# Attention in rounds of two tiles: four shared score accumulators, and the shared work laid out anew over the steps

## The reference, cut to what matters

```
y = layernorm(x1)                          # 512 x 512
q, k = y @ Wq, y @ Wk                      # 8 heads of 64 columns
gl_v, gl_o = y @ Ws, y @ Wd                # 8 heads x 5 experts each
wv   = top2_mask(gl_v) * sigmoid(gl_v)
v    = sum over e of wv[..., e] * (y @ Wv[e])        # 8 heads x 64
attn = softmax(q * 64**-0.5 @ k.T) @ v
out  = sum over e of top2_mask(gl_o)[..., e] * attn @ Wo[e]
x    = x1 + tanh(g) * out
```

## Time and profile before

| | us |
|---|---|
| median of 3 runs | 1353.11 |
| the profiled execution | 1354.09 |
| its span | 1352.3 |
| PE busy in the span | 1245.2 |
| DVE busy | 855.2 |
| POOL busy | 696.3 |
| ACT busy | 638.3 |

### The profile page before, as it was taken

One profiled execution on the slowest core, in us unless ns is written; L12 is line 12 of the kernel. 1 busy time (PEld: TensorE's weight loads), 2 busy tenths in 40 slices (PEclk: granted clock), 3 DMA queues, 4 the chain that ended last, 5 costly groups with the idle time before them and its releaser, 6 DMA issues.

```text
span 1352.3 us, 20097 instructions
## 1 busy us (share of the span) xinstructions
PE 1245.2 (92%) x6376; PEld 909.4 (67%) x6376; DVE 855.2 (63%) x1587; ACT 638.3 (47%) x1402; POOL 696.3 (51%) x499
## 2 busy tenths in 40 slices
PE   3899999999999997889899999999999999999985
PEld 2688888888888876656566566576576575675653
DVE  5677776868777562754755765666666566466453
ACT  3343443434344323455545555555554554564551
POOL 2524242434424242654863963963954945955853
PEclk8799999999999998999999999999999999999997
DMA  6231313223131233001010010010020020010010
GB/s 221 74 110 47 116 62 100 93 94 109 47 116 39 86 141 110 19 0 32 1 63 31 0 62 31 0 62 31 0 90 3 8 85 0 8 54 0 23 39 32
DMA packets 40713, 75.73 MB, mean 56 GB/s; under 512 B 3760, under 2 KB 4272, under 8 KB 40688
## 3 DMA queue, kind: packets, MB, share of 16 engines
q1 hardware_dynamic: 40688, 75.42, 16.7%
HBM read 58.63 MB, written 16.78 MB: 56 GB/s over the span
## 4 chain that ended last, share of the span: by engine, by line
PE 36%; POOL 15%; issue 5%; DVE 3%; ACT 1%; POOLq 1%; DVEq 0%; ACTq 0%
PE ps_r L1577 7%; PE ps_r L1589 6%; POOL v_acc L1171 5%; PE ps_o L1652 5%; PE ps_p L1640 5%; PE ps_s L1629 5%; PE ps_r L1612 5%; POOL spare L1165 4%; POOL z L1183 4%; POOL v_acc L1165 1%; PE ps_r L1566 1%; PE ps_r L1603 1%; DVE sig L1434 1%; DVE nmax L1348 1%; PE ps_r L1596 0%
## 5 line engine op out<-in xcount | busy, mean ns | idle before, releaser
L1348 DVE TENSOR_REDUCE nmax<-ps_s 128x1 f32<-128x512 f32 x256 | 173.9, 685 | 207.3 <-PE ps_s L1629 207.2
L1226 ACT ACTIVATE probs<-ps_s,nmax 128x512 f32<-128x512 f32 x256 | 176.4, 689 | 262.0 <-DVE nmax L1348 259.3
L1183 POOL TENSOR_TENSOR z<-z,z_tmp 128x1280 f32<-128x1280 f32 x56 | 163.7, 2923 | 155.3 <-DVE z_tmp L1362 142.7
L1171 POOL TENSOR_TENSOR v_acc<-v_acc,spare 128x512 f32<-128x512 f32 x128 | 165.7, 1294 | 10.0
L1629 PE MATMUL ps_s<-k,q 64*128 64x512 f32 x768 | 123.7, 426 | 47.1 <-ACT probs L1226 45.6
L1640 PEld LDWEIGHTS ps_p<-ident,probs 128*128 128x128 f32 x1024 | 115.5, 142 | 73.0 <-issue 52.5
L1640 PE MATMUL ps_p<-ident,probs 128*128 128x128 f32 x1024 | 160.2, 283 | 1.7 <-ACT pt L1235 1.7
L1235 ACT ACTIVATE pt<-ps_p 128x512 f32<-128x512 f32 x256 | 151.9, 594 | 3.6 <-PE ps_p L1640 3.6
L1165 POOL TENSOR_TENSOR spare<-xv,pick 128x512 f32<-128x512 f32 x128 | 136.3, 1065 | 10.0
L1629 PEld LDWEIGHTS ps_s<-k,q 64*128 64x128 f32 x768 | 62.5, 185 | 101.6 <-ACT probs L1226 60.1
L1652 PE MATMUL ps_o<-pt,v_acc 128*64 128x512 f32 x512 | 130.6, 611 | 0.2 <-ACT pt L1235 0.2
(11 more groups left out here) (165 smaller groups left out, 2196.7 us busy)
## 6 DMA issues: line engine op xcount, KB each, us to landing
stage<-in_x SPq DMA_DIRECT2D x32, 256.0 KB, 3.1
stage<-in_ctx SPq DMA_DIRECT2D x32, 256.0 KB, 2.7
x_sb<-in_x SPq DMA_DIRECT2D x8, 1024.0 KB, 5.2
x_dram<-x_sb SPq DMA_DIRECT2D x32, 256.0 KB, 2.0
stage<-x_dram SPq DMA_DIRECT2D x8, 1024.0 KB, 5.6
spare<-x_dram SPq DMA_DIRECT2D x8, 1024.0 KB, 5.7
out_dram<-spare SPq DMA_DIRECT2D x32, 256.0 KB, 2.0
stage<-in_ctx_t SPq DMA_DIRECT2D x28, 256.0 KB, 3.3
```

Source lines behind the costliest of these rows:

```text
L1171: pool.tensor_tensor(acc, acc, v_tmp[:], ALU.add).then_inc(v_steps, 1)
L1183: pool.tensor_tensor(zv, zv, z_tmp[:, h % 2], ALU.add).then_inc(z_pool, 1)
L1226: act.activation(probs[:, n % PROBS, :], ps_s[:, n % 2, :], ACT.Exp, bias=nmax[:, n:n + 1], accum_out=den[:, h, t:t + 1]).then_inc(p_exp, 1)
L1348: dve.tensor_reduce(nmax[:, n:n + 1], ps_s[:, n % 2, :], AX_X, ALU.max, negate=True).then_inc(nmax_ready, 1)
```

## The change

All is in `expert_attention`. What it does:

- `ps_p` goes; `ps_s` has four banks, one a tile. A tile's transposed exponentials are written into the bank that held its scores. Scores wait until the copies of the tiles two rounds before are done (`pt_ready`), no more for an exponential.
- A round is two steps. On even n PE issues `scores(n)`, then the transposes of tiles n-2 and n-1, ACT the copies of n-2 and n-1 and then the exponentials of n and n+1, and DVE the maxima of n and n+1, all at the head of the step. On odd n there is only shared work.
- `values` is one block of 16 matmuls at step 12 of the pair.
- The tables of shared parts are new. High parts are taken in the step in which a part ends, low parts always in the odd step of the round.
- Gates: one `compare` for both kinds, 8 larger operations at step 1 with other slices, one count over both at step 2, and all of `route_values` at step 3.
- POOL: all `mix_values` of a batch, then the sums of heads 1 to 5. The sums of heads 6 and 7 go to DVE (`mix_sum`), at steps 41 and 42; `turn_z` is at step 43 and waits for these.

```diff
-    TURN_Y_AT = [-11, -11, -10, -9]
-    EXPERTS_AT = [[-9], [-8, -7], [-5, -4], [-3]]
-    Q_AT = [[-6, -6], [1, 2], [6, 6], [18, 18]]
-    K_AT = [[-3, -2], [3, 4], [10, 10], [19, 19]]
-    PV_AT = [11, 12, 12, 13]
-    TURN_O_AT = [17, 25, 34, 41]
-    TURN_Z_AT = [45, 45, 45]
-    RESULT_AT = [[46], [47], [47, 48], [49]]
+    TURN_Y_AT = [-11, -11, -10, -10]
+    EXPERTS_AT = [[-9], [-8], [-2], [-1, 0]]
+    Q_AT = [[-6, -5], [1, 2], [7, 8], [17]]
+    K_AT = [[-3], [3, 6], [9, 10], [18, 19]]
+    PV_AT = 12
+    TURN_O_AT = [16, 23, 31, 39]
+    TURN_Z_AT = [43, 43, 43]
+    RESULT_AT = [[45], [46], [47], [48]]
     NORMALISE_AT = -13
-    GATES_AT = -3
-    ROUTE_AT = [-1, -1]
-    MASK_AT = 1
+    GATES_AT = 1
+    ROUTE_AT = 3
     MIX_PLACES = [(1, 1), (2, 0)]
+    LAST_SUMS = [(2, 1), (3, 0)]
+    BANKS = 4
...
-                if n or not first:
-                    pe.wait_ge(p_exp, b * STEPS + n)
+                if n >= BANKS or not first:
+                    pe.wait_ge(pt_ready, b * STEPS + n + 2 - BANKS)
...
-                if part == 1 and 0 <= n - LAG < STEPS:
-                    turn_probs(b, n - LAG, first)
+                if part == 1 and n % 2 == 0:
+                    for before in (n - 2, n - 1):
+                        if 0 <= before < STEPS:
+                            turn_probs(b, before)
...
+            def batch(b, first=False):
+                for p in range(PAIRS):
+                    mix_values(b, p, first)
+                for p in range(LAST_PAIR):
+                    mix_sums(b, p)
...
+            def mix_sum(b, h):
+                dve.wait_ge(z_dve, b * H + h + 1)
+                if h == 2 * LAST_PAIR:
+                    dve.wait_ge(z_pool, (b + 1) * POOL_SUMS)
+                else:
+                    dve.wait_ge(z_ready, b * 2 + 1)
+                zv = z[:].rearrange("p t (e k) -> p t e k", e=E)
+                dve.tensor_tensor(zv, zv, z_tmp[:, h % 2], ALU.add).then_inc(z_ready, 1)
...
+            def compare(b):
+                dve.wait_ge(logits_ready, b * NT + NT)
+                both = logits[:].rearrange("p s g e -> p (s g) e")
+                square = beaten[:].rearrange("p g k j -> p g (k j)")
+                for d in range(1, E):
+                    early, late = both[:, :, 0:E - d], both[:, :, d:E]
+                    for first_place, other, than, order in ((d, late, early, ALU.is_gt), (d * E, early, late, ALU.is_ge)):
+                        places = square[:, :, bass.ds(first_place, E - d, step=E + 1)]
+                        dve.tensor_tensor(places, other, than, order).then_inc(compared, 1)
```

More of the change, by code:

```diff
@@ L925, in ended, with lo_behind @@
         return [what[:2] for what in parts_at(n) if what[2] == what[3] - 1]
-    def steps_behind(behind, name, i):
-        return behind.get(name + "0", 1) if name in "qk" and i == 0 else behind.get(name, 1)
+    def lo_behind(n):
+        return 1 - n % 2
     RING = 3
@@ L1035, in expert_attention @@
         z_pool = sem("z_pool")
+        z_ready = sem("z_ready")
         zt_ps = sem("zt_ps")
@@ L1280, in step @@
                             out_copy(b, p, first)
[L1281 to L1284, removed]
-                    return
[L1286 to L1291, removed]
+                    if n % 2 == 0:
+                        for before in (n - 2, n - 1):
+                            if 0 <= before < STEPS:
+                                probs_copy(b, before, first)
+                        for tile in (n, n + 1):
+                            if 0 <= tile < STEPS:
+                                scores_exp(b, tile, first)
+                    return
+                for name, i in ended(n):
+                    part_hi(b, name, i, first)
                 if n == NORMALISE_AT:
@@ L1299, in _ @@
             for n in range(EARLY - STEPS, EARLY):
-                for part in range(3):
+                for part in range(2):
                     step(0, n, part, True)
@@ L1460, in step @@
                     for what in ended(n - behind):
-                        if behind == steps_behind(LO_BEHIND, *what):
+                        if behind == lo_behind(n - behind):
                             part_lo(b, *what)
                 if part == 3:
[L1464 to L1469, removed]
+                    if n == GATES_AT:
+                        compare(b)
+                    if n == GATES_AT + 1:
+                        count_better(b)
                         count_values(b)
-                    if n == ROUTE_AT[1]:
+                    if n == ROUTE_AT:
                         route_values(b, first)
[L1473 to L1476, removed]
                     if n == NORMALISE_AT:
@@ L1632, in scores, with turn_probs, values @@
                             end.then_inc(s_ready, 1)
-            def turn_probs(b, n, first):
+            def turn_probs(b, n):
                 pe.wait_ge(p_exp, b * STEPS + n + 1)
-                if n >= 2 or not first:
-                    pe.wait_ge(pt_ready, b * STEPS + n - 1)
                 for k in range(NT):
-                    end = pe.transpose(ps_p[:, n % 2, k, :], probs[:, n % PROBS, k * P:(k + 1) * P], ident[:])
+                    end = pe.transpose(ps_s[:, n % BANKS, k * P:(k + 1) * P], probs[:, n % BANKS, k * P:(k + 1) * P],
+                                       ident[:])
                 end.then_inc(pt_ps, 1)
[L1643 to L1655, removed]
+            def values(b, p, first):
+                pe.wait_ge(pt_ready, b * STEPS + PAIR * p + PAIR)
+                pe.wait_ge(v_steps, (b * PAIRS + p + 1) * V_STEPS)
+                if p or not first:
+                    pe.wait_ge(o_ready, b * PAIRS + p)
+                for k in range(NT):
+                    for a in range(2):
+                        end = pe.matmul(ps_o[head_rows(a), :], v_acc[:, p, k, a, :], pt[:, p % 2 * 2 + a, k, :],
+                                        start=k == 0, stop=k == NT - 1)
+                end.then_inc(o_ps, 1)
             def step(b, n, part, first=False, last=False):
@@ L1660, in step @@
                     scores(b, n, first)
[L1661 to L1662 removed]
+                if part == 1 and n % 2 == 0:
+                    for before in (n - 2, n - 1):
+                        if 0 <= before < STEPS:
+                            turn_probs(b, before)
                 if part == 2:
                     for p in range(PAIRS):
[L1665 to L1667 removed]
+                        if n == PAIR * p + PV_AT:
+                            values(b, p, first)
                     for what in parts_at(n):
```

91 lines of the change are left out of this document (35 added, 56 removed).

## The result

The change made the kernel slower: 1389.81 us (median of 4 runs, 1388.45 to 1393.8) against 1352.82 in the same comparison, a ratio of 1.0276 with a 95% interval of 1.0251 to 1.0300. I had forecast 1340 and given 1308 to 1364.

What follows compares the result with a forecast made beforehand. PE was taken as the bound, busy 92.6 of 98.1 us a batch. Terms 4.1 - 10 - 2 - 2.8 - 2.6 = -13.3 from 1353.1 gave 1340 us, range 1308 to 1364.

Steps and rivals of the forecast that it cites:

- PE work, 90.0 us a batch: Second half, steady batch: PE work falls from 92.6 to 90.0 us, by joined values groups and fewer interruptions.
- rival 3: The PE work doesn't shrink, a batch stays at 92.6 us of it: 1359 us, chance 0.13.
- All three waits of scores for exponentials go: Second half: with four score banks all three pauses of scores go, 4.5 us a batch.
- The gates: Steps 0 to 4: comparisons on DVE delay maxima and exponentials, so PE pauses 3.8 us, then loses 0.25.
- 2.6 us undisturbed: Gates on DVE: time of the 8 comparisons of 1280 elements without POOL beside them.
- turn_z: Steps 8 to 11: PE pauses 3.45 us at turn_z for two DVE sums of 2.0 us each; 0.96 before.
- turn_o of pair 1, "0.3 late": It takes the bank of the third transposes of y, whose low part ends 0.3 us late.
- The sum: Steady batch 97.8 us against 98.1; from first batch's scores(30) to last batch's scores(12), 629.3 against 625.2.
- The first batch: Scores 0 to 30 of the first batch: 77 us against 87.2 before, -10.
- the last: Last batch, scores(12) to the last values: 53.8 us against 56.6 before, -2.8.
- The slower one: Rival 1: turn_z waits longer for DVE sums, 4.35 us each, up to 1373 us, middle 1363; chance 0.24.
- Rival 2: Comparisons and sums hardly wait for POOL, pauses of 0 and 2.25 us: 1303 us; chance 0.20.

Runs made afterwards that it cites:

- e9: e7 with the value gates counted and routed at step 5 in place of 7, the mask's count left at 7; 1284.1 us, ratio 0.9487.
- e1: The changed kernel with the comparisons cut as before the change (one expert against the others, output contiguous), at the same step; 1380.8 us, ratio 1.0201.
- e7: The changed kernel with gates spread over steps 3 to 7, transposes of pair 1 at 24, sums at 43 and 44, turn_z at 45; 1336.1 us.
- e2: The changed kernel, but POOL begins its sums of heads 4 and 5 only when the next batch's comparisons are done; 1346.4 us, ratio 0.9962.
- e10: The changed kernel with idle-running matmuls on PE filling all three pauses (step 4, before turn_z, before the experts); 1375.6 us, ratio 1.0171.

## Why the prediction was wrong

- **PE work, 90.0 us a batch: right.** e9 measures 89.85 for 92.62 before: 2.8 us were saved where 2.6 were summed. So rival 3 did not come. The Trainium skill (TensorE: Matmul & The Clock Gate, "Step-by-step: what each phase is for") says that weight loads are pulled ahead of matmuls in flight; that joined groups would then save next to nothing was drawn from it in the prediction, and this is what the runs do not bear out. The two effects in it, values in one block and fewer groups of transposes, were not run apart.
- **All three waits of scores for exponentials go: right.** In the kernel after, PE's rows for scores have no such wait.
- **The gates: the mechanism right, the size wrong.** The block between the maxima makes transposes at step 4 wait for the exponential of tile 3. The term mis-sized is "2.6 us undisturbed": 5.05, since I took the rate of the earlier trace rows for operations whose output had another step. (The two rates that I give there make 2.2, not 2.6; that e1 measures 2.60 is luck in part.) POOL's share was right: it added 3.9 us to the 5.05, as it was to add 3.9 to the 2.6. Where I had `compare` end 6.5 us after it begins, it took 8.5. The pause was 5.2 and not 3.8 (plus 0.25).
- **turn_z: right**, 3.5 us on average for 3.45 (2.9 to 4.2). I took 2.0 us for each sum; the first took 1.5 to 2.5 from batch to batch, the second 1.9.
- **turn_o of pair 1, "0.3 late": wrong, 2.0.** I had the experts in front of the transposes at step 23. The loop issues the late step of batch b before the early one of b+1, so `turn_o` is first and the experts get the bank that isn't read yet.
- **The clock: the term that was missing, and the largest.** The sum put down every pause at its own length. The earlier trace rows show the clock at 1.00 with pauses of up to 1.6 us; nothing there shows one of 5. But the earlier trace rows did: behind a pause of 8.4 us `turn_z` took 2.79 us, and 1.53 in the earlier trace rows. I had both rows and did not ask why they differ. In the kernel after, behind 5.2 us, 16 values matmuls took 5.7 us for 3.65. All in all it is 5.1 us a batch, where the sum has nothing.
- **The sum.** 97.8 forecast, 105.8 measured: 1.2 from the gates, 1.7 from the order, 5.1 from the clock. From scores(30) of the first batch to scores(12) of the last it is 682.2 us where I had 629.3, and that is the whole miss. The first batch (79.6 for 77), the last (52.3 for 53.8) and the end (11.1 for 10.9) came within 2.6 us, and their errors nearly cancel.
- **The rivals.** The slower one was in the wrong place: it priced the sums on DVE, and named a wait of over 5.4 us at `turn_z`. The loss came from terms that I held for settled. Rival 2 put the kernel without the gates' pause and with a shorter one at `turn_z` at 1303; e9, where the experts' pause is gone too, takes 1284.

## What to carry to other kernels

On an engine that bounds the kernel, price a pause of some us by what runs behind it too: here the pauses of a batch, 10.9 us, cost another 5.1 us of PE time at a lower clock, of which 2.7 came back when they were filled. A row in which the same work takes longer behind a pause is the place to read this from. An operation's rate holds for its access pattern and no further; a new step in the output is a new operation. And when pauses are removed, check each producer's lead again, since the next one was 5 us behind (e7), and the order in which two interleaved batches issue the same step.

## What the runs showed of the hardware

- A comparison of 256 results on DVE, 2 bytes each, in groups of four with a step of six elements takes 1.15 us, and 0.48 us with the four side by side (first batch, POOL idle); all eight take 5.05 us, and 2.66 with the same inputs and outputs side by side.
- The granted clock stayed at 1.00 over pauses of up to 1.6 us, two of them 5 us apart (before), and was 0.60 in the 7.3 us behind one of 5.2. For pauses of 2 us it went either way: in the kernel after the experts' block was slowed behind 2.0 us in some batches and not in others, in e2 in all six middle batches, while in the same six batches `turn_z` never was, behind 2.1 us. The batches of the kernel after differ by up to 3.7 us (103.6 to 107.3); those of the kernels without a fall (before, e9, e10) repeat within 0.1.
- DVE and POOL hold each other up in both directions. Beside POOL's two sums the eight comparisons took 8.92 us, and 5.05 once POOL had to wait (e2). POOL's operation that began right behind the start of a DVE sum took 2.32 us in place of 1.06 (988.37, beside the sum at 988.29):

```profile
988.37 2.32 POOL L1157 TENSOR_TENSOR spare<-xv,pick 128x512 f32<-128x512 f32 x1
```
